# Taking PSUM outputs out by a ScalarE copy and a GpSimd addition in an attention and expert block

## What is computed

```python
h = _layernorm(x) * (1 + ca) + sa
x = x + ga * attn(h)                      # 16 heads of 16, softmax over 1024 keys
h = _layernorm(x) * (1 + cb) + sb
base = h @ W_base + b_base
# for each of 8 experts: losses = mean((relu(h @ W_enc + b_enc) @ W_dec + b_dec - h) ** 2)
adp = connected_idx[argmin(losses)]
mid = relu(h @ W_down[adp] + b_down[adp])
x = x + gb * (base + mid @ W_up[adp] + b_up[adp])
```

## Time and profile before

| | us |
|---|---|
| median of 3 runs | 980.05 (978.15 to 981.6) |
| the profiled execution | 980.53 |
| its span from first to last instruction | 978.7 |
| mean granted TensorE clock | 0.983 |

### The profile page before, as it was taken

How to read it: one execution, slowest core, us unless ns; L and a number is a source line. 1 busy time by engine, 2 the same in 40 slices (tenths; PEclk the granted TensorE clock), 3 DMA queues, 4 the chain that set the end, 5 groups by cost and what they waited for, 6 DMA issues and landing times.

```text
span 978.7 us, 16476 instructions
## 1 busy us (share of the span) xinstructions
PE 945.7 (97%) x5794; PEld 475.7 (49%) x5794; DVE 793.5 (81%) x1629; ACT 657.7 (67%) x1295; POOL 335.8 (34%) x447
## 2 busy tenths in 40 slices
PE   6999999989999999999999999999999999999998
PEld 4444344434344355544454455445445465644486
DVE  4789988978888787887788888778878888888365
ACT  2148887877786777666668786766657867566930
POOL 4050234124364343111456543410165613116320
PEclk9889999999999899999999999999999999999999
DMA  6932061342525311416342411405434321132001
GB/s 180 144 73 39 23 110 46 61 93 73 94 49 89 60 36 35 77 27 110 99 105 50 87 35 46 75 14 88 127 82 83 52 36 36 39 98 79 30 6 49
DMA packets 47890, 66.93 MB, mean 68 GB/s; under 512 B 12139, under 2 KB 32112, under 8 KB 47796
## 3 DMA queue, kind: packets, MB, share of 16 engines
q1 hardware_dynamic: 46572, 65.00, 31.4%
q0 software_dynamic: 384, 0.79, 0.6%
q10 hardware_dynamic: 852, 0.09, 0.1%
HBM read 27.48 MB, written 12.59 MB: 41 GB/s over the span
## 4 chain that ended last, share of the span: by engine, by line
PE 75%; DVE 10%; DMA 5%; SPq 4%; ACT 2%; issue 2%; POOL 2%; ACTq 0%; DVEq 0%; POOLq 0%
PE pE L813 23%; PE pM L813 22%; PE pO L813 20%; PE pX L813 8%; DVE mx L1298 7%; SPq L1880 2%; DMA QO<-lo 1%; DMA xin<-in_x 1%; DMA QO<-mT 1%; ACT P L1120 1%; DMA outs<-osb 1%; PE pM L907 1%; ACT h1T L1161 1%; DVE junk L1435 1%; SPq L1938 1%
## 5 line engine op out<-in xcount | busy, mean ns | idle before, releaser
L1298 DVE TENSOR_REDUCE mx<-pE 128x1 f32<-128x512 f32 x440 | 287.2, 683 | 48.7 <-PE pE L813 47.4
L1298 DVE TENSOR_REDUCE mx<-pM 128x1 f32<-128x512 f32 x447 | 294.4, 683 | 31.2 <-PE pM L813 29.6
L1120 ACT ACTIVATE P<-pM 128x512 f32<-128x512 f32 x457 | 260.9, 602 | 69.2 <-PE pM L813 67.7
L1120 ACT ACTIVATE P<-pE 128x512 f32<-128x512 f32 x431 | 243.3, 602 | 86.9 <-PE pE L813 85.8
L813 PE MATMUL pO<-P,V 128*17 128x512 f32 x2048 | 261.7, 607 | 1.2 <-ACT osb L1127 1.0
L813 PE MATMUL pM<-KO,QO 48*128 48x512 f32 x447 | 178.7, 446 | 4.1 <-DMA QO<-lo 3.6
L813 PE MATMUL pM<-QO,KO 50*128 50x512 f32 x457 | 178.6, 435 | 1.0
L813 PE MATMUL pE<-KO,QO 48*128 48x512 f32 x440 | 175.0, 447 | 3.3 <-DVE mx L1298 2.5
L813 PE MATMUL pE<-QO,KO 50*128 50x512 f32 x431 | 166.2, 437 | 3.5 <-DMA QO<-mT 3.0
L813 PEld LDWEIGHTS pM<-QO,KO 50*128 50x128 f32 x457 | 80.8, 187 | 101.4 <-issue 70.8
L813 PEld LDWEIGHTS pE<-QO,KO 50*128 50x128 f32 x431 | 76.0, 187 | 99.4 <-issue 75.7
(11 more groups left out here) (303 smaller groups left out, 1323.0 us busy)
## 6 DMA issues: line engine op xcount, KB each, us to landing
outs<-osb SPq DMA_DIRECT2D x31, 256.0 KB, 2.2
KO<-hi SPq DMA_DIRECT2D x56, 128.0 KB, 4.0
QO<-hi SPq DMA_DIRECT2D x56, 128.0 KB, 5.6
x<-in_x SPq DMA_DIRECT2D x20, 256.0 KB, 3.5
out<-x SPq DMA_DIRECT2D x16, 256.0 KB, 2.1
AT<-outs SPq DMA_DIRECT2D x15, 256.0 KB
asum<-wsum SPq DMA_DIRECT2D x15, 256.0 KB
KO<-lo SPq DMA_DIRECT2D x28, 128.0 KB, 3.7
```

The source lines that it names most:

```text
L1120: e.activation(P[:, u % 3, j, :], bank(s), ACT.Exp).then_inc(*empties(s))
L1298: e.tensor_reduce(mx[:, hq % 2, k:k + 1, kh], bank(s), AX.X, ALU.max, negate=True).then_inc(*empties(s))
```

## The change

In batches 0, 1 and 2 VectorE no longer takes the banks of `out` and `base`. ScalarE copies the bank to a new buffer `xadd` in SBUF and frees it; GpSimd then adds `xadd` to the rows in `x2`. A semaphore `s_added` counts these additions, 16 in all (8 `out` in batches 0 and 1, 4 `base` and 4 `out` in batch 2). There is one `xadd`, so ScalarE waits before each copy for the addition before it, and SyncE waits with a finished tile for its addition. Batch 3 (`LAST`) stays as it was. The space that GpSimd's own transfers have for their descriptors is halved.

```diff
+        xadd = sb("xadd", [128, 512])
...
+        sums_of = [x for x, piece in map(step, S.list) if x[0] in ("out", "base") and piece and x[1] < LAST]
+
+        def added(s):
+
+            return sums_of.index(s) + 1
...
+                elif kind in ("out", "base") and last and s[1] < LAST:
+                    act.wait_ge(*full(*s))
+                    act.wait_ge(s_added, added(s) - 1)
+                    e.activation(xadd[:, :], bank(s), ACT.Copy).then_inc(*empties(s))
...
-                elif kind == "base" and last:
+                elif kind == "base" and last and s[1] == LAST:
...
-                elif kind == "out" and last:
+                elif kind == "out" and last and s[1] == LAST:
...
+                elif kind in ("out", "base") and piece and s[1] < LAST:
+                    b, k = s[1:]
+                    sl = x2[:, 2 * k:2 * k + 2, :].rearrange("p t n -> p (t n)")
+                    pool.wait_ge(*emptied(*s))
+                    if kind == "out" and b in PARTED:
+                        pool.wait_ge(s_added, added(("base", b, k)))
+                    e.tensor_tensor(sl, xadd[:, :], sl, ALU.add).then_inc(s_added, 1)
...
-                    sp.wait_ge(*emptied(*s))
+                    sp.wait_ge(*((s_added, added(s)) if b < LAST else emptied(*s)))
...
-    nc = bacc.Bacc("TRN2", target_bir_lowering=False, num_devices=1, dynamic_dma_scratch_size=4096)
+    nc = bacc.Bacc("TRN2", target_bir_lowering=False, num_devices=1, dynamic_dma_scratch_size=2048)
```

## The result

The changed kernel takes 992.8 us in the median (990.8 to 996.6), the kernel before 980.2. The ratio is 1.0132, with an interval of 1.0107 to 1.0157. Measured again beside more executions of before (experiment e18_after_again), the ratio is 1.0116 (1.0096 to 1.0135). So the change costs 11 to 13 us. The profiled execution of the changed kernel shown here took 996.56 us, with a span of 994.5. It is the longest of the four: it was already 3.8 us behind the profile of before ahead of the first changed step, so places are compared by differences, not by absolute times.

What follows compares the result with a forecast made beforehand. TensorE, busy 97%, was taken as the bound, with queue order deciding. 4.0 (a) + 2.3 (b) + 3.5 (c) + 2.4 (d) + 2 x 1.4 (e) + 1.0 copies - 2.0 relief = 14.0 us, giving 994.0; range 984.0 to 1004.0.

Steps and rivals of the forecast that it cites:

- rival 1: The queues hold, as forecast: 994; chance 0.70.
- (b): Batch 1, second out: rows of mturn 24 wait for the addition behind prep 2; standstill 3.3 us, 2.3 in the sum.
- (c): Batch 0, second out: rows of mturn 16 wait for the addition behind prep 1; standstill 4.5 us, 3.5 in the sum.
- (a): Batch 2, base: second copy waits for GpSimd's addition behind fetch 2; TensorE stands 5.0 us, 4.0 in the sum.
- L: Landing time of the rows SyncE sends for mturn 16 and 24: 3.0 us, ends 1.5 and 4.2.
- (d): Batch 2, last two outs: second copy waits for the addition, exponentials and SyncE's rows late; 2.4 us, bounds 0.5 to 4.5.
- (e): TensorE's clock is low after a standstill: 1.4 us more for each of (a) and (b), nothing for (c).
- (f): Smaller scratch for GpSimd's own transfers, such as the twelve KO transfers at the start: 0 us, bounds 0 to 4.8.
- Copies and relief: Sixteen ScalarE copies push exponentials back, 1.0 us; VectorE relieved of sixteen additions gains TensorE 2.0 us.
- Rival 2: The same waits, largely made good, with only (a) left whole: 7 us, 987; chance 0.13.
- Rival 3: GpSimd's additions and VectorE's line 1435 get into each other's way: 1002; chance 0.09.
- Rival 4: Faster: VectorE's lateness at the pE maxima is the real bound, and (a) to (d) are covered: 975; chance 0.04.

Runs made afterwards that it cites:

- e18_after_again: The changed kernel itself, unaltered, measured again in more executions beside before: 993.0 us, ratio 1.0116.
- e15_store_behind: Changed kernel with batch 2 undone, and SyncE's stores of tiles 0 1 and 1 1 moved behind the rows of mturn 16 and 24: 981.3 us, ratio 1.0002.
- e5_scratch: Kernel before with only the scratch for GpSimd's transfers halved, 4096 to 2048: 980.6 us, ratio 0.9981.
- e13_one_of_d: e6_order with only out 2 3, the second of two neighbouring outs, back on VectorE: 981.1 us, ratio 0.9995.
- e1: Changed kernel with the four base additions of batch 2 back on VectorE: 987.2 us, ratio 1.0048.
- e6_order: Changed kernel with fetch 2, prep 1, prep 2 moved behind additions base 2 1, out 0 1, out 1 1 in GpSimd's queue: 983.9 us, ratio 1.0015.
- e16_d_store: e6_order with SyncE's stores of tiles 2 2 and 2 3 moved behind the rows of mturn 30: 982.8 us, ratio 1.0028.
- e7_order_no_d: e6_order with the last two outs of batch 2 (2 2 and 2 3) back on VectorE: 980.2 us, ratio 0.9988.
- e17_no_add: e7_order_no_d with GpSimd's fourteen additions left out and ScalarE copying one column only, sums missing from the result: 980.2 us, ratio 0.9987.
- e5b_scratch: Kernel before with only the halved scratch, measured once more: 979.8 us, ratio 0.9986.

## Why the forecast held, point by point

The forecast was 994.0, and 992.8 was measured. The likeliest case came, rival 1. But that the sum came so close is in part luck: against the lags of e18_after_again, (b) and (c) with their clock were 4.1 us too large, (a) with its clock 1.3 too small, and copies and relief together 1.0 too small.

**(a), right in its mechanism, under-sized.** Standstill 5.0 forecast, 4.79 seen. The 1.0 taken off for what the others catch up was wrong: stretch (a) costs 6.7, which is 4.79 plus 1.9, and the clock's part is 2.1 by the rows, so only 0.2 was made good. TensorE did not wait for VectorE at this place before, so there was nothing to give back. 6.7 against 4.0 + 1.4.

**(b) and (c), right in their mechanism, over-sized.** The steps were as forecast: `prep`, addition, store, rows, TensorE. Three terms were off. First L: 1.98 and 1.96 us in place of 3.0. The forecast took it from transfers that land in 3.0 us at best; it had named 1.5 as the low end. The Trainium skill, "DMA: Bandwidth & Descriptors", "Anatomy of one DMA", gives a fixed cost of about 2.0 us for a small transfer of GpSimd's kind; the rows sent by SyncE, with 1.96 to 1.98 us, agree with that number here. Second, `prep` itself started earlier than before, 478.06 less 3.8 of lag behind the profile of before = 474.2 against 475.12 there, since its last input landed sooner once the rows were held back (that the rows' transfers had slowed it is argued, not shown). Third, more was made good than 1.0 each, by the waits for VectorE that vanish (e15_store_behind). In (b) TensorE was in its products with P until 715.46, so it stood for 0.90 only, and the clock stayed at 1.00; the 1.4 for it was wrong:

```profile
716.00:720.00 4.00, 3.23 (x10) 1.32 (x10) 3.90 (x10) 1.79 (x3) 1.33 (x1) 1.00 0.40 121
```

In (c), where nothing was added for the clock "since it stood at 0.65 already", the step failed: that low clock is in no profile with the small scratch and the rows in time, so it could not be counted on (e5_scratch). In e18_after_again the stretch 480 to 484 reads

```profile
480.00:484.00 4.00, 4.00 (x20) 1.14 (x22) 3.21 (x9) 2.56 (x5) 1.88 (x3) 0.57 0.24 71
```

which is 1.7 us lost, with 2.27 us of standstill before it; 2.3 remains of 4.0. Together (b) and (c) cost 3 where 5.8 + 1.4 stood in the sum. Against the one profile of before, which lost 2.0 in the same two stretches, it is 1.

**(d), about right, for half of the reason.** 2.4 forecast, 2.2 to 4.0 by the lags, 2.7 by the ratios. ScalarE's wait for the buffer is in it (e13_one_of_d), with 0.7 to 1.2 us of standstill and, in e1 and e6, 1.7 of low clock right behind. The delay of SyncE's rows, named beside it, is not (e16_d_store); the later `asum` is, with 0.6 us in the changed kernel, and the forecast didn't name it. The 4.0 of the first profile holds 1.7 of low clock near 920 us that e18_after_again doesn't have.

**(e), the wrong rule.** A fixed 1.4 per standstill does not hold: 2.1 behind 4.79 us, 3.2 behind 3.01, 1.7 behind 2.3, none behind 0.90. And 0.94 us were followed by 1.7 in e6_order, 0.96 us at the same place by none in e18_after_again.

**(f) right**: no cost, rather a gain of some 1.6 us. **Copies and relief**: + 1.0 and - 2.0 were both nothing (e7_order_no_d, e17_no_add). The forecast's 2.0 leant on direct waits of 1.5 us and on maxima being late behind the additions. The waits did shrink in the changed kernel, to 14.5 and 14.1, but mostly in the gaps it made: it has none between 478 and 504 and between 709 and 734, where e5b_scratch has 1.6 and 0.9 at the same steps.

**The rivals.** Rival 2, largely made good with only (a) left, was half true for (b), and not for (d). Rival 3, collisions: they exist. In e18_after_again, line 1448 (1435 before) took 1.22 us beside an added addition and 0.43 the next time, alone:

```profile
885.47 1.28 POOL L1796 TENSOR_TENSOR x<-xadd,x 128x512 f32<-128x512 f32 x1
885.81 1.22 DVE L1448 CUSTOM_DVE_ANT_0 junk<-wd,bc 128x256 f32<-128x256 f32 x1
...
887.07 0.43 DVE L1448 CUSTOM_DVE_ANT_0 junk<-wd,bc 128x256 f32<-128x256 f32 x1
```

But three of its sixteen took over 1 us in before, and three in the changed kernel and in e17_no_add too. VectorE's busy time with GpSimd's fourteen additions and without them (e7_order_no_d, e17_no_add) differs by 1.1 us, and the time not at all:

```profile
PE 944.7 (97%) x5794; PEld 475.8 (49%) x5794; DVE 786.1 (80%) x1615; ACT 663.8 (68%) x1309; POOL 352.7 (36%) x461
```

```profile
PE 943.2 (97%) x5794; PEld 476.4 (49%) x5794; DVE 785.0 (80%) x1615; ACT 659.1 (68%) x1309; POOL 335.2 (34%) x447
```

The Trainium skill's rule in "SBUF — State Buffer", "Who interferes with whom", that such an operation and a GpSimd read exclude each other, fits the long instruction, and it doesn't set the time. Rival 4, faster, falls with e17_no_add: there is no gain to be had from taking these additions off VectorE. VectorE's maxima still keep weight loads waiting for 33 us in e17_no_add, and no experiment here relieved those. Rival 5 came true only for e7_order_no_d, with the waits removed.

VectorE's busy time fell by 7.2 us, not by 11. In a row of its operations each starts about 0.6 us after the one before while it lasts 0.69 (in before, 463.27 the addition and 463.88 the maximum behind it), so each removed one is less than 0.69 of busy time (16 x 0.6 = 9.6); the rest is open.

## What to carry to other kernels

Moving work to an engine with room is first of all a question of what stands ahead of it in that engine's queue: sixteen additions that cost 1.5 us in one order cost 11 to 13 in another, behind a step that waits for a transfer. A single hand-over buffer makes the producer wait for the consumer's whole operation wherever two come close together. And before a second engine is relieved, price it by leaving its work out: here that showed that nothing was to be gained from these additions.

## What the hardware did that I had not expected

The low clock behind a gap doesn't scale with the gap: a shorter standstill (3.01 us) lost more to it than a longer one (4.79), 3.2 us against 2.1, because more work ran while the clock was low. Two executions of the same kernel also differ by a low clock at places that no change touches. In the first profile of the changed kernel it stood at 0.69 and 0.88 in the two stretches behind 920 us, where TensorE was busy throughout, and at 1.00 in e18_after_again:

```profile
920.00:924.00 4.00, 4.00 (x19) 0.80 (x18) 1.52 (x1) 3.03 (x8) 2.70 (x3) 0.69 0.21 69
924.00:928.00 4.00, 4.00 (x20) 2.17 (x16) 1.12 (x2) 2.72 (x7) 1.08 (x1) 0.88 0.00 1
```

```profile
920.00:924.00 4.00, 4.00 (x24) 1.39 (x23) 2.42 (x5) 4.00 (x10) 0.10 (x1) 1.00 0.00 0
```

That is worth 1.7 us, and a stall read from a single profile may therefore belong to that execution. And in both profiles of the changed kernel, four times, TensorE starts 1.96 to 1.98 us after SyncE sent the first rows of QO.
